# Self attention on Trainium2 in groups of four units, with each next batch's value projection made inside it

## What is computed

```python
def proj(W): return (X @ W.T).reshape(b, n, H, 2 * dh).transpose(0, 2, 1, 3)
Q, K, V = (proj(Wq), proj(Wk), proj(Wv))
Q1, Q2 = jnp.split(Q, 2, axis=-1)
K1, K2 = jnp.split(K, 2, axis=-1)
A1 = jnp.where(causal, jnp.einsum('bhnd,bhmd->bhnm', Q1, K1) * scaling, -jnp.inf)
A2 = jnp.where(causal, jnp.einsum('bhnd,bhmd->bhnm', Q2, K2) * scaling, -jnp.inf)
attn = jax.nn.softmax(A1, axis=-1) - lam * jax.nn.softmax(A2, axis=-1)
O = jnp.einsum('bhnm,bhmd->bhnd', attn, V)
rms = jnp.sqrt(jnp.mean(O * O, axis=-1, keepdims=True) + EPS)
O = O / rms * rms_scale * (1.0 - LAMBDA_INIT)
return Oc @ Wo.T        # Oc: the heads of O side by side, added to x afterwards
```

## Time and profile before

| | |
|---|---|
| median of three executions | 1783.49 us (1781.65 to 1785.44) |
| the profiled execution | 1781.16 us, span 1779.4 us |
| PE, PEld | busy 95%, 78% of the span |
| DVE, ACT, POOL | 67%, 54%, 39% |
| Q and K projections | about 1230 to 1338 us of the span |
| value projections | about 1338 to 1384 us |
| attention | about 1384 to 1571 us |
| experts | about 1571 to 1779 us |

### The profile page before, as it was taken

How to read it: one execution, slowest core, us unless ns; L and a number is a source line. 1 busy time by engine, 2 the same in 40 slices (tenths; PEclk the granted TensorE clock), 3 DMA queues, 4 the chain that set the end, 5 groups by cost and what they waited for, 6 DMA issues and landing times. The chain is left out here.

```text
span 1779.4 us, 37801 instructions
## 1 busy us (share of the span) xinstructions
PE 1692.6 (95%) x15755; PEld 1381.9 (78%) x15770; DVE 1198.7 (67%) x1625; ACT 962.8 (54%) x1479; POOL 694.7 (39%) x313
## 2 busy tenths in 40 slices
PE   7999999999999999999999999668999799879999
PEld 6788888888888888888888887567888566658886
DVE  5137787887887878778788788777233777752223
ACT  4337666666666666666666666653221788720000
POOL 0003555555555555555555554002000566632220
PEclk9999999999999999999999999778999999999999
DMA  5211111111111011111111100125662333311101
GB/s 189 65 48 28 40 43 28 40 30 41 40 30 41 31 38 43 28 40 40 31 40 29 42 16 27 54 61 182 185 176 71 95 96 94 94 29 61 53 0 47
DMA packets 105079, 105.26 MB, mean 59 GB/s; under 512 B 8027, under 2 KB 73563, under 8 KB 104931
## 3 DMA queue, kind: packets, MB, share of 16 engines
q1 hardware_dynamic: 104930, 103.09, 19.8%
HBM read 80.00 MB, written 23.07 MB: 58 GB/s over the span
## 5 line engine op out<-in xcount | busy, mean ns | idle before, releaser
L632 POOL TENSOR_TENSOR b_acc<-b_acc,b_s 128x1024 f32<-128x1024 f32 x168 | 459.1, 2733 | 258.0 <-ACT b_s L840 247.4
L869 DVE TENSOR_TENSOR b_s<-b_s,b_mb 128x2048 f32<-128x2048 f32 x128 | 365.5, 2857 | 3.9 <-ACT b_mb L823 3.9
L907 DVE TENSOR_TENSOR b_mx<-b_psS,b_mx 128x512 f32<-128x512 f32 x480 | 331.1, 690 | 51.5 <-PE b_psS L704 38.3
L840 ACT ACTIVATE b_s<-b_s 128x2048 f32<-128x2048 f32 x128 | 245.2, 1916 | 82.4 <-DVE b_s L869 82.4
L849 ACT ACTIVATE b_s<-b_psS 128x2048 f32<-128x2048 f32 x128 | 240.8, 1881 | 68.6 <-DVE b_mx L907 68.6
L43 PE MATMUL b_work<-wvT,cT 128*128 128x512 f32 x496 | 203.1, 409 | 0.0
L43 PE MATMUL b_work<-cT,wkT 128*128 128x512 f32 x496 | 200.3, 404 | 0.0
L45 PE MATMUL b_work<-wvT,cT 128*128 128x512 f32 x496 | 194.2, 391 | 0.0
L45 PE MATMUL b_work<-cT,wkT 128*128 128x512 f32 x496 | 193.7, 390 | 0.0
L44 PE MATMUL b_work<-wvT,cT 128*128 128x512 f32 x496 | 193.5, 390 | 0.0
L44 PE MATMUL b_work<-cT,wkT 128*128 128x512 f32 x496 | 193.5, 390 | 0.0
(11 more groups left out here) (245 smaller groups left out, 3114.8 us busy)
## 6 DMA issues: line engine op xcount, KB each, us to landing
cin<-in_ctx SPq DMA_DIRECT2D x64, 512.0 KB, 3.7
q_scratch<-d_st SPq DMA_DIRECT2D x32, 256.0 KB, 2.8
k_scratch<-d_st SPq DMA_DIRECT2D x32, 256.0 KB, 2.8
e_q<-q_scratch SPq DMA_DIRECT2D x16, 512.0 KB, 3.7
k_sb<-k_scratch SPq DMA_DIRECT2D x64, 128.0 KB, 3.9
experts_sb<-in_L_ffn_expert_w SPq DMA_DIRECT2D x8, 1024.0 KB, 5.4
b_kT<-in_x SPq DMA_DIRECT2D x4, 512.0 KB, 8.2
q_scratch<-a_q SPq DMA_DIRECT2D x8, 256.0 KB, 2.3
```

Source lines behind the costliest of these rows:

```text
L632: nc.gpsimd.tensor_tensor(acc[:, :, :], acc[:, :, :], s[:, buf, 2 * i:2 * i + 2, :], ALU.add).then_inc(sum_done, 1)
L840: nc.scalar.activation(part, part, ACT.Exp, scale=SCALE).then_inc(exp_done, 1)
L869: nc.vector.tensor_tensor(s[:, n % BUFS, :, :], s[:, n % BUFS, :, :], mb[:, :].rearrange("p (o n) -> p o n", o=1).broadcast_to([P, CHUNK, ...
L907: nc.vector.tensor_tensor(mx[:, :, :], part, mx[:, :, :], ALU.max).then_inc(mx_done, 1)
```

## The change

It does five things.

1. A unit's scores are made by float32 matmuls of 32 rows by 128 columns, one for each of its four maps (PE uses four row groups of the array), instead of three full products with a block diagonal. Q and K are therefore stored whole, not as high and low parts: DVE alone empties the bank (scaled by minus the softmax scale for Q), one DMA stores it, `k2` needs no zeros, and a half batch loads with two DMAs in place of five.
2. Four units go together, as one *half* of a batch. `psS` is one set of four banks, bank j holding map j of the four units. DVE takes the minimum of the negated scores, in three reductions (map 0, map 1, maps 2 and 3 together). ACT makes 16 exponentials in two halves of eight.
3. The first softmax isn't normed. DVE makes one factor lambda x sum0 / sum1 for each head and adds the second map times it to the first (`weigh`: three small operations, then four of 128x128). The norm of the outputs takes it up through the square of the sum (`es`). POOL no longer multiplies maps. It squares the outputs and makes the whole Newton step.
4. The values of batch 0 alone are made in `self_projections`. Those of batch b+1 are made by PE in the second half of batch b of the attention, in two products of twelve matmuls into `psW`, emptied by ACT and DVE.
5. All batches are written out; the engines' loop over 3 to 7 is gone. Some buffers move (`oT`, the experts' weights, `k2`, `sm`).

The core of the diff. PE's new functions and its order of a half:

```diff
+            def scores(b, hf):
+                pe.wait_ge(qk_in[hf], b * 32 + 32)
+                for u in range(N):
+                    for j in range(HG):
+                        rows = slice(j * HD, (j + 1) * HD)
+                        last = nc.tensor.matmul(psS[:, j, u, :], q2[rows, hf, u, :], k2[rows, hf, u, :],
+                                                start=False, stop=u == N - 1)
+                last.then_inc(s_full, 1)
...
+            def outputs(b, hf, turned):
+
+                p = 1 - hf
+
+                reached(pe, o_copied, b * 2 + (hf - 2))
+                if turned:
+                    pe.wait_ge(w_lo, b * 2 + (hf - 4))
...
             def batch(b, front, back, out, end):
...
+                for hf in range(2):
+                    before = back if hf == 0 else front
                     if front:
...
+                        masks(b, hf, (0, 1))
+                    if before:
+                        turn_maps(b, hf, 0)
+                    if end and hf == 1:
+                        project(b, (6, 7))
+                    if front:
+                        masks(b, hf, (2, 3))
+                        scores(b, hf)
+                    if end and hf == 0:
+                        project(b, (0, 1, 2, 3))
+                    if values_left(b, front) and hf == 1:
+                        values(b, 0, end)
+                    if before:
+                        turn_maps(b, hf, 1)
+                    if out:
+                        turn_outputs(b, hf, back)
+                    if before:
+                        outputs(b, hf, end if hf == 0 else out)
+                    if end and hf == 0:
+                        project(b, (4, 5))
+                    if values_left(b, front) and hf == 1:
+                        values(b, 1, end)
```

`project` multiplies by Wo, three matmuls for each k; `values` is 12 matmuls. ACT's half is, in this order: `exponentials(0)`, the copy of the second turned pair of the half before, in half 1 the copy of the first values, `exponentials(1)`, the copy of the first turned pair of this half, the copy of four units of outputs, the high part of the turned outputs. DVE's half:

```diff
+                    if front:
+                        dve.wait_ge(s_full, b * 2 + (hf + 1))
+                        lowest(hf, slice(0, 1))
+                        lowest(hf, slice(1, 2))
+                    if back if hf == 0 else front:
+
+
+                        weigh(b, hf - 1, 1 - hf, 1)
+
+                        reached(dve, norm_step, b * 12 + (6 * hf - 17))
+                        nc.vector.scalar_tensor_tensor(
+                            out=es[:, eight(1 - hf)].rearrange("p (u i) -> p i u", i=2), in0=sums[:, 1 - hf, :, 0, :],
+                            scalar=EPS * 2 * HD, in1=sums[:, 1 - hf, :, 0, :], op0=ALU.mult,
+                            op1=ALU.mult).then_inc(es_done, 1)
+                    if front:
+                        lowest(hf, slice(2, 4))
+                    if end if hf == 0 else out:
+
+                        p = 1 - hf
+                        dve.wait_ge(w_hi, b * 2 + (hf - 4))
+                        nc.vector.scalar_tensor_tensor(
+                            out=oT[1][:, 4 * p:4 * p + 4, :].rearrange("p k t -> p (k t)"), in0=psO[p][:, :],
+                            scalar=rs[:, 0:1], in1=f32(oT[0][:, 4 * p:4 * p + 4, :]).rearrange("p k t -> p (k t)"),
+                            op0=ALU.mult, op1=ALU.subtract).then_inc(w_lo, 1)
+                    if front:
+                        weigh(b, hf, hf, 0)
```

## The result

The changed kernel takes 1761.31 us, the median of four executions (1760.65 to 1763.10), against 1783.43 (1781.65 to 1785.44, four) of the kernel before: a ratio of 0.9879, 95% interval 0.9865 to 0.9892. It is faster by 22 us, where 27 were predicted. The profiled execution took 1760.7 us, with a span of 1758.9.

What follows compares the result with a forecast made beforehand. PE nearly bounds the attention (18.7 of 21.0 us a batch). Starting at 1344.9, its last scores end at 1512.1 and experts start at 1543.0, not 1571.5: -28.5, +1.6 for the clock, in all -27, so 1756.5; range 1738 to 1776.

Steps and rivals of the forecast that it cites:

- the new wait: Full halves of the attention: PE's products of outputs wait 1.1 us for w_lo, which DVE counts only after oT.
- Values moved: Stage before the attention, PE working alone: 14 of 16 value products leave it, -39.4 us; SP's first loads cost nothing.
- The full half: Attention: ten halves with Wo, turned outputs and the new wait take 11.8 us each, 118 in all.
- The first five intervals: Attention's start, halves without Wo, turned outputs and the wait: 8.0 us, 10.65 twice and 8.85 twice.
- The drain: From the end of the last scores to the experts' start: 29.5 us with statistics, then 1.4.
- one term of 1.6 us: First two halves of the attention: one stretch at the lower PE clock after gaps, +1.6 us.
- B: Rival, chance 0.15: no wait for oT, so ten halves and the end lose 1.1 us less; 1744.5.
- C: Rival, chance 0.20: DVE's es held up by POOL's scaling, 1.04 us later in 11 halves; +11.4, so 1768.
- D: Rival, 0.10 with similar endings: scores' row groups don't overlap, 3.5 instead of 1.27 us in 16 halves; +36, so 1792.
- The groups only shift the waits: Rival, chance 0.05: unpriced small operations and semaphores cost 1.5 us more per half, no difference left; about 1781.

Runs made afterwards that it cites:

- The kernel that keeps PE busy: Against the changed kernel: low part of oT made before the large minimum, plus unread matmuls in four halves including the fifth and last; 1749.07 us.
- PE kept busy in head and drain: Against the changed kernel: unread matmuls added behind the first scores, those of batch 1 and the last ones; 1759.99 us.
- the values ahead: Against the changed kernel: all sixteen value products made ahead of the attention, none in it; 1802.08 us.
- low part late: Against the changed kernel: DVE makes oT's low part behind the weighing of the present half instead of ahead of it; 1814.88 us.

## Why the prediction was right

The direction, the part of the values and the new wait were right; what the clock does behind a gap was priced too low. The size was 4.8 us short between the medians, and 6.5 between the profiled executions (1754.2 forecast, 1760.7 measured). Step by step:

- **Values moved, -39.4.** Right. PE alone works 7 us instead of 46, and PE's first instruction of the attention stands at 1343.39, 1.5 us ahead of the plan; nearly all of that was there before the changed part. The loads cost nothing, as taken.
- **The full half, 11.8.** Measured 12.09, so 118 became 120.9. By its parts, counted from T, the end of the half's scores: the four additions of `weigh` took 0.26 from start to start, not 0.2, so the turned outputs end at T+4.1 instead of 3.7; `oT` was released as computed, and `outputs` begins at T+4.9 (4.85). Sixteen products take 1.78 to the next start, not 1.55; the twelve behind them 2.89, not 2.8; masks and turned maps 1.4, not 1.3; the scores 1.10, not 1.27. PE's gap was 0.82 instead of 1.1 us, and all of it lay on the path: taking it away gave back 1.05.
- **The first five intervals, 47.0.** Measured 49.7. The three that are longer (9.37, 11.62 and 9.42 for 8.0, 10.65 and 8.85) hold stretches at the lower clock, the other two agree with the plan to 0.3 (where the exponentials set the end, 8.62 for 8.85: the forecast's own terms, 3.6 + 0.6 + 8 x 0.34, give 6.9 where it says 7.1). The kernel that keeps PE busy has 46.6. The forecast had one term of 1.6 us for this; the stretch cost 3.1.
- **The drain, 29.5 + 1.4.** This is the step that failed by most: 36.1 from the end of the last scores (T) at 1516.0. PE waits 2.91 us for the weighed maps (1518.95), and the clock falls: the second turned maps end at 13.7 instead of 10.5, and POOL ends the last scaling at 25.0 instead of 22.5. With PE kept busy in head and drain it ends at 23.2, so some 1.8 of these 2.5 us are the clock's. The rest is POOL, which ends the last square 1.5 us late in both, out of the chain of the half before, less 0.7 that the power and the small operations behind it took less. Two terms were left out: the turning (1542.86) waits 1.9 us for Wo's products of the batch before, which PE's order puts ahead of it, and between turning and Wo stands the splitting of `oT`, 1.1 us. The power and POOL's small operations, the unpriced rows, took 3.1 us, from 1536.80 to 1539.94, for 3.8.
- **Balance.** -1.6 at the start, +2.7, +2.9 and +5.2 make 9.2, against the 1543.0 of the forecast; less the term of 1.6, and less 1.1 us that the experts are shorter (206.8 for 207.9), 6.5. In the experts the split products of the earlier trace rows take 6.4 us instead of 8.0, since the lower clock came earlier, while x is turned (0.50 from 1557 to 1562), and was over by then. The early start and the shorter experts, 2.7 us together, are luck: no part of the forecast says them, and without them it would have been 9 us short.

Of the rivals: B (no wait) was wrong as a case of this kernel, and roughly right as a price: without the wait the kernel takes 1753.3, or about 1751.3 with the changed kernel's start, where 1744.5 was given. 4.8 us of the difference are the forecast's own, and 2 are the price: 10 us for the 12 given. C didn't happen: `es` took 0.16 us in all sixteen halves, DVE was first each time. (The row that C goes by is a product of 128x4, L1533, not an addition; the argument needs only its two inputs in SBUF.) The lock showed elsewhere, in `lsum`. D was false, and its price for the order that does it is 1.65 us a half, not 2.2. "The groups only shift the waits" holds in one sense: without the values inside, the rest of the change gains nothing.

What the forecast didn't see is why the values cost so little. It charged them as PE time in a half that waits anyway. In truth the first twelve hold the clock up. The expectation ahead of that experiment shows it: it gave the halves without values some 8.9 us, and they took 11.79.

## What to carry to other kernels

When work is moved into a stage with gaps, price the gap twice: as a place to hide work in, and as what the clock does behind it. PE's idle time can be worth filling even with unread work, and taking useful work out of such a gap can make a kernel slower. In a pipeline written out by hand, look for the one wait that everything of the fullest engine is queued behind, and ask what its releaser does just before: moving 0.7 us of DVE ahead of 1.2 us of DVE was worth 8 us. And price the drain by each engine's order, not only by the chain: of its missing terms one was matmuls queued ahead (1.9 us), the other a link of the chain itself (1.1 us).

## What was not expected of the hardware

- The clock fell again and again in the middle of the attention, behind waits of 2.9 us (with the values ahead) and 3.1 us (low part late), in each such full half. Behind the 0.82 us of the changed kernel's full halves it never did.
- A wait of the same length in the same place need not bring it down: 2.92 us before 1389.5 in the changed kernel left it at 1.00, 2.92 us before 1386.4 in the kernel with PE kept busy was followed by 0.50 (1390 to 1393). What decides between them stays open. Here, filling the gaps ahead of it moved the fall into this one.
- A fall costs nearly as much again as the wait it stands behind: with the low part late, 1.7 us on sixteen products of 128x64 and 1 us on what follows, behind a wait of 3.1.
- DVE's operation on 128x4 with both inputs in SBUF took 0.13 us alone, 0.27 when POOL's square had 0.25 us left, and 0.92 when it had 0.9 left; both times it ended with POOL's.
